# State-space layer: GpSimd prepares the last two channel blocks' step products in units 3 and 5 of the round that uses them, instead of in units 0 and 1

## The reference

```python
xz = h @ W_in.T;  xi, z = split(xz)
xc = silu(causal_conv(xi))                      # 512 channels
dbc = xc @ W_x.T;  delta, Bm, Cm = split(dbc)   # 64 + 16 + 16
delta  = softplus(delta @ W_dt.T + b_dt)
deltaA = exp(delta[..., None] * A)              # 16 states a channel
BX     = (delta * xc)[..., None] * Bm           # (delta * xc) is the step product
hs     = scan(deltaA, BX)                       # h[t] = deltaA[t] * h[t-1] + BX[t]
y = sum_n(hs * Cm) + D * xc
x = x + (y * silu(z)) @ W_out.T
```

## Time and profile before

| | |
|---|---|
| three runs | 1289.67, 1286.73, 1289.17 us; median 1289.17 |
| the profiled execution | 1286.74 us, its span 1285.0 us |
| busy, share of the span | PE 88%, DVE 82%, ACT 64%, POOL 60% |
| the chain that ended last, by engine | PE 42%, DVE 33%, ACT 10%, POOL 8%, issue 7% |
| mean granted TensorE clock | 0.949 |
| the state-space part | about 366 to 1053 us; rounds 1 to 7 start near 447, 533, 619, 707, 793, 881 and 967 us |

### The profile page before, as it was taken

The page is one execution under the profiler, slowest core; times in us unless marked ns, Lnnn a source line. Parts: engine busy times, 40 slices in busy tenths (PEclk is TensorE's granted clock), DMA queues, the critical chain, the costliest instruction groups (busy, mean ns, idle before and its releaser), DMA issues.

```text
span 1285.0 us, 17476 instructions
## 1 busy us (share of the span) xinstructions
PE 1128.5 (88%) x5960; PEld 660.0 (51%) x5960; DVE 1050.3 (82%) x1642; ACT 825.1 (64%) x1816; POOL 775.4 (60%) x641
## 2 busy tenths in 40 slices
PE   7798888879759998998998999989989689999974
PEld 3455555544325454554554545545545346666643
DVE  4577777675689999999999999999999985676657
ACT  1455555655466786777767767877776436788763
POOL 6001111100389898998998999989989952554202
PEclk9899999998979999999998999989999899999878
DMA  7000002000510600502404107014042003100000
GB/s 211 13 13 13 13 13 73 2 1 3 201 44 0 217 34 2 205 17 88 162 1 181 42 1 251 1 54 168 1 150 88 1 11 90 34 18 18 2 1 26
DMA packets 22141, 79.13 MB, mean 62 GB/s; under 512 B 4935, under 2 KB 8847, under 8 KB 21138
## 3 DMA queue, kind: packets, MB, share of 16 engines
q1 hardware_dynamic: 22054, 78.02, 17.7%
HBM read 76.77 MB, written 1.24 MB: 61 GB/s over the span
## 4 chain that ended last, share of the span: by engine, by line
PE 42%; DVE 33%; ACT 10%; POOL 8%; issue 7%; DMA 0%; DVEq 0%; SPq 0%; POOLq 0%; ACTq 0%
PE ps L675 38%; DVE ps L2089 10%; DVE arena L2094 6%; DVE arena L2092 5%; POOL arena L2003 4%; PE ps L744 4%; ACT ps L1886 2%; DVE hstat L1213 2%; POOL arena L2015 2%; DVE arena L2052 2%; ACT L670 1%; DVE arena L1189 1%; ACT arena L936 1%; DVE arena L1179 1%; ACT arena L1776 1%
## 5 line engine op out<-in xcount | busy, mean ns | idle before, releaser
L675 PE MATMUL ps<-arena 128*32 128x100 f32 (+10 forms) x3330 | 517.4, 380 | 67.3 <-ACT arena L936 14.6
L2003 POOL TENSOR_TENSOR arena<-arena 128x1600 f32<-128x1600 f32 x128 | 456.6, 3582 | 34.0 <-DVE ps L2089 25.8
L675 PE MATMUL ps<-arena,ident 128*128 128x400 f32 x1024 | 386.5, 528 | 29.4 <-POOL arena L2015 19.9
L675 PEld LDWEIGHTS ps<-arena 128*32 128x32 f32 (+7 forms) x3330 | 259.4, 144 | 294.3 <-issue 115.9
L1886 ACT ACTIVATE ps<-arena 128x400 f32<-128x400 f32 x512 | 282.9, 589 | 184.5 <-DVE arena L2092 151.3
L2089 DVE TENSOR_TENSOR_SCAN ps<-ps,arena 128x800 f32<-128x800 f32 x176 | 320.6, 1822 | 22.8 <-ACT ps L1886 17.1
L675 PEld LDWEIGHTS ps<-arena,ident 128*128 128x128 f32 x1024 | 201.5, 200 | 196.4 <-issue 28.3
L642 POOL TENSOR_SCALAR stat<-stat 100x1 f32<-100x1 f32 (+1 forms) x44 | 8.5, 193 | 419.9 <-DVE stat L623 419.0
L2092 DVE TENSOR_TENSOR arena<-ps,arena 128x800 f32<-128x800 f32 x176 | 174.5, 991 | 6.0
L2015 POOL TENSOR_TENSOR arena<-arena 128x1600 f32<-128x1600 f32 x40 | 143.1, 3579 | 16.8 <-DVE arena L2094 16.7
L2094 DVE TENSOR_TENSOR_SCAN arena<-ps,arena 128x800 f32<-128x800 f32 x80 | 140.3, 1803 | 0.9 <-ACT ps L1886 0.7
(11 more groups left out here) (199 smaller groups left out, 1025.7 us busy)
## 6 DMA issues: line engine op xcount, KB each, us to landing
arena<-bc_scratch SPq DMA_DIRECT2D x64, 800.0 KB, 6.4
arena<-in_ctxT SPq DMA_DIRECT2D x16, 361.0 KB, 4.0
arena<-in_w_in SPq DMA_DIRECT2D x4, 1024.0 KB, 5.0
arena<-in_expT SPq DMA_DIRECT2D x1, 2048.0 KB, 12.9
arena<-in_w_out SPq DMA_DIRECT2D x4, 512.0 KB, 3.2
arena<-in_mask SPq DMA_DIRECT2D x8, 141.0 KB
arena<-in_xT SPq DMA_DIRECT2D x2, 400.0 KB, 4.1
x_tok<-in_x_tok SPq DMA_DIRECT2D x1, 800.0 KB
```

The lines of the kernel that those rows point to most:

```text
L675: return nc.tensor.matmul(outp, lhsT, rhs, start=first, stop=last)
L2003: nc.gpsimd.tensor_tensor(bx[:, unit % BX].rearrange("p (j t) -> p j t", j=SEGMENT), bbc[:, nq].rearrange("p (j t) -> p j t", j=SEGMENT), ...
```

## The change

Two numbers of `AT` change; nothing is added or taken away.

```diff
     "aA": 10,
     "gA": 15,
-    "gD": (14, 15, 16, 17),
+    "gD": (14, 15, 19, 21),
     "vY": (5, 10, 13, 16),
```

## The result

The changed kernel took 1281.01 us (median of 22 runs, 1277.73 to 1285.67), the kernel before 1285.43 us (22 runs, 1281.41 to 1289.67). The ratio is 0.9969, with a 95% interval of 0.9958 to 0.9981: 0.31% faster, some 4 us, where 0.26% slower was forecast.

What follows compares the result with a forecast made beforehand. VectorE was taken as the bound, GpSimd close behind. Costs of 0.72 + 0.81 + 1.82 = 3.35 us, added to the three-run median, gave 1292.5 us, 0.26% more; range 1288.7 to 1295.7 us.

Steps and rivals of the forecast that it cites:

- The units that are relieved: Units 0 and 1 on GpSimd: the 2.4 us freed before unit 3's scan input becomes idle time; gain nothing.
- The loaded units: Units 3 and 5 on GpSimd: each added pair's 1.18 us delays what follows, from unit 5's and unit 7's inputs on.
- Unit 7, even rounds: Rounds 2, 4, 6: VectorE starts unit 7 0.24 us later a round, 0.72 us in three rounds.
- The norm's root, odd rounds: Rounds 1, 3, 5: late `gm_rstd` delays ScalarE's scaling and unit 7's decays, 0.27 us a round, 0.81 us in all.
- Round 7: Last round: late GpSimd inputs delay VectorE's units 6, 7 and 10, costing 1.82 us by unit 10.
- Rival 1: VectorE's waits for ScalarE hide GpSimd's lateness; only the last round pays, 1.2 to 1.8 us: 1290.7 us, chance 0.15.
- What else is late, and its cover: Unit 9's product with C is 2.36 us late; TensorE's idle 2.45 us covers its sum by 0.2 us, no cost.
- A rule weighed: TensorE's clock: TensorE's 1.2 GHz stretches after idle time: the first idle stretch moves some 3 us earlier, same length; sum unchanged.
- Rival 2: TensorE's clock falls at another time; odd rounds' gate product waits, 3 x 1.21 = 3.63 us, come back: 1288.9 us, chance 0.13.
- The signs of being wrong: Two signs in the trace after: VectorE's waits for GpSimd do not rise, or the L2110 waits change.
- The base: Median of three runs of the kernel before, to which the 3.35 us sum was added, giving 1292.5 us.

Runs made afterwards that it cites:

- the filled pair: The kernel before and the changed kernel, each with 12 zero matrix products a round added on TensorE in rounds 0 to 6: ratios 0.9959 and 0.9963.
- the filled kernel before: The kernel before with 12 zero matrix products a round added on TensorE in units 11 and 12 of rounds 0 to 6: ratio 0.9959, 1277.83 us.
- the two profiles of before: The unchanged kernel before, profiled in two separate executions: 1286.74 us in the first and 1281.0 us in the second.
- second profile of after: The changed kernel, unedited, profiled once more: 1284.5 us in one execution.
- unit 11 filled: The kernel before with only 8 zero products a round on TensorE, ahead of the sum of unit 9 in rounds 0 to 6: ratio 0.9997.

## Why the prediction was wrong

- *The units that are relieved.* Right. GpSimd's idle time ahead of unit 3's scan input and unit 1's product grew (in round 7 from 0.21 and 1.49 us to 1.94 and 1.66), and the filled pair shows no gain from it. (The loaded units open with a small misreading, that GpSimd works without a pause from 971.99: the next row has 1.49 us of idle time. The added pairs come behind it, so no term hangs on it.)
- *Unit 7, even rounds,* forecast 0.24 us. The step from an even round's first gate product to the next one's grew by 0.19 us (85.48 to 85.67) in the filled pair. In the trace after, unit 7 of round 2 starts 4.10 us behind the gate product (571.48 - 567.38), before 3.92.
- *The norm's root, odd rounds,* forecast 0.27 us, measured 0.19 (86.34 to 86.53). It shows at unit 6 and not at unit 7, as a wait of VectorE for ScalarE that was not there before; the wait at unit 7 stays 0.65 us, where 0.9 was forecast:

```profile
481.61 3.54 DVE L2094 TENSOR_TENSOR_SCAN arena<-ps,arena 128x800 f32<-128x800 f32 x2 [0.21 <-ACT ps L1886]
```

- *Round 7,* forecast 1.82 us, measured 1.69. Rival 1, that the delays are absorbed, did not come true: the sum was 2.85 us of 3.35.
- *What else is late, and its cover.* Here is the step that failed. "The idle time covers it" is right for VectorE's waits, and the late sum of unit 9 kept nobody waiting. But the step took TensorE's idle time as free to move.
- *A rule weighed: TensorE's clock.* The failing sentence is "the change moves the first idle stretch some 3 us earlier without changing its length, so the sum stays as it is". The idle stretch ahead of the sum of unit 9 was a place where the clock could fall. When it falls there, that sum is 1.75 us longer (4.60 and not 2.85), and takes time from the next idle stretch, the 1.86 us ahead of the step products (0.96 us left in round 1, 0.16 in round 2). The falls on the step products and the sum of unit 11, which cost VectorE 6.8 us in six rounds, then stay away in rounds 1, 2, 5 and 6, and are short in rounds 3 and 4: 0.6 us in all. So 6.1 us came back where the sum put the clock at nothing, and 6.1 against 2.85 us is the gain of 3.27 us in the rounds. The median over the runs gained 4.4 us; the other 1.1 us are not accounted for. Rival 2 named this mechanism, at 0.13 and at 3 x 1.21 = 3.63 us, 40% too small, because it priced only the wait of the gate product. The low clock also made ScalarE's softplus late: VectorE's wait for the decays of unit 15 was 1.27 us at 701.86 in round 3, and in round 1 after it waits there only 0.24 us at 530.90, for GpSimd's scan input. In the filled kernel before, a round has that 0.24 us and 0.27 us at the fourth gate product, which rounds with a long fall have not; 1.21 + 1.27 - 0.24 - 0.27 = 1.97 us is the price of a long fall that the rounds show. And even rounds, whose fall is short, lost something too (85.78 and 85.48 filled).
- *The signs of being wrong.* The second came: the L2110 waits changed. The first did not, but most of the rise of the waits for GpSimd does not come from its lateness (above).
- *The base.* The forecast stood on a median of three runs, 1289.17 us; over 22 runs it is 1285.43. That adds 3.7 us to the miss of the absolute time and nothing to that of the change.

The Trainium skill's sentence that the clock's watch runs freely against the kernel (TensorE: Matmul & The Clock Gate, Part 1: The HAM clock gate) agrees with the two profiles of before, in which the long falls sit in odd and in even rounds.

What stays open: why a stretch of 1.86 us brings the fall in most rounds and not in all, and why it is long or short. In round 3 after, the idle time ahead of the step products is 1.86 us as before, yet the fall is short; that round alone is 1.45 us of the 4.96, and the late sum as explained here does not account for it. In the second profile of after, round 3, the sum of unit 9 waited 1.89 us and the step products 1.86 us, and both ran at full clock.

## What to carry to other kernels

When TensorE has short idle stretches in a loop, ask what stands right behind each: an idle stretch ahead of work that another engine waits for can cost a clock fall on that work (1.96 us for a long one here), and a stretch ahead of work with slack cost nothing when the fall was short, and about 1 us when it was long and the sum 3.5 us late. A delay that is fully covered on the timeline can therefore make a kernel faster, and the gain belongs to the clock and not to the edit; filling TensorE's idle time in both versions shows what the edit itself does. Here that gave the better kernel too: the old order, with TensorE kept busy.

## What was not expected of the hardware

- Sums of four products take 2.85 us at 2.4 GHz and 5.70 us when all of it falls in the 1.2 GHz stretch; a fall lasted some 3.4 us in the cheap rounds and 6.8 us in the costly ones.
- In a profile of before, the falls repeat with the rounds: in the first at 512, 686 and 860 us (rounds 1, 3, 5) and, shorter, at 601, 775 and 949 us (rounds 2, 4, 6), each 174 us after the last of its kind. In the second the long ones are at 592, 767 and 941 us. Other kernels do not keep a pattern: with unit 11 filled the long falls came in rounds 0, 1, 4 and 6. One profile shows one pattern.
- Eight small products of zeros in a 1.9 us gap are worth 0.5% of the whole kernel.
